# Two narrow attentions of a four-layer transformer: raw bank copied once, units turned in pairs, first sequences prepared in the stage before

## The reference, cut to what matters

```python
# layer 1: one k and v of 8 columns, shared by the 16 heads
latent = x @ Wc_down; q = (latent @ Wq_up).reshape(B, T, 16, 8)
k, v = split(latent @ Wkv_up)                    # causal softmax(q k / sqrt 8) @ v, then @ Wc_proj
# layer 3: k and v for every head, causal and no further back than 128 tokens
q, k, v = split(x @ w_in.T + b_in, 3)            # 16 heads of 8
allowed = (j <= i) & (j >= i - 128)
return (softmax(where(allowed, q k / sqrt 8, -1e9)) @ v) @ w_out.T + b_out
```

## Time and profile before

| | |
|---|---|
| three timed runs | 2560.18 us median (2559.87 to 2560.31) |
| the profiled execution | 2552.11 us, its span in the trace 2550.4 us |
| PE busy over the span | 92% |
| DVE, ACT, POOL busy | 63%, 58%, 63% |
| TensorE clock granted, mean | 0.976 |
| stage 2, last output of stage 1 to its own last output | about 858 to 1157 us |
| stage 6, likewise | about 2168 to 2503 us |

### The profile page before, as it was taken

How to read it: one execution, slowest core, us unless ns; L and a number is a source line. 1 busy time by engine, 2 the same in 40 slices (tenths; PEclk the granted TensorE clock), 3 DMA queues, 4 the chain that set the end, 5 groups by cost and what they waited for, 6 DMA issues and landing times. The chain is left out here.

```text
span 2550.4 us, 61619 instructions
## 1 busy us (share of the span) xinstructions
PE 2348.4 (92%) x23721; PEld 1820.9 (71%) x23721; DVE 1604.4 (63%) x4234; ACT 1470.3 (58%) x3038; POOL 1595.8 (63%) x2569
## 2 busy tenths in 40 slices
PE   6999999999998699988999999999999968788897
PEld 5888888888886366656777788777877757455555
DVE  5666666666664277774455477777777622577776
ACT  5666666666664377764444466666656523466665
POOL 6888888888884444443333277777777722566664
PEclk8999999999999789999999999999999989899999
DMA  8930000000000100001000000000000045000000
GB/s 295 328 129 2 2 2 2 2 2 2 2 2 1 40 7 2 2 2 33 1 1 1 3 4 4 6 6 6 4 6 6 4 145 172 15 10 8 8 4 34
DMA packets 22915, 82.91 MB, mean 33 GB/s; under 512 B 3969, under 2 KB 10882, under 8 KB 21602
## 3 DMA queue, kind: packets, MB, share of 16 engines
q1 hardware_dynamic: 19474, 71.76, 8.8%
q0 software_dynamic: 3152, 7.21, 0.9%
HBM read 71.76 MB, written 46.79 MB: 46 GB/s over the span
## 5 line engine op out<-in xcount | busy, mean ns | idle before, releaser
L978 POOL TENSOR_TENSOR XR<-XR,T 128x256 f32<-128x256 f32 x504 | 369.0, 732 | 36.9 <-DVE T L858 7.3
L722 ACT ACTIVATE P<-ps 128x384 f32<-128x384 f32 (+1 forms) x512 | 250.7, 542 | 179.9 <-PE ps L2691 178.4
L2691 PE MATMUL ps<-P,V 128*64 128x256 f32 (+3 forms) x4096 | 332.0, 345 | 9.2 <-DVE O L1482 7.9
L1466 DVE TENSOR_REDUCE bm<-ps 128x3 f32<-128x384 f32 x512 | 260.0, 549 | 105.5 <-PE ps L2691 104.6
L2691 PEld LDWEIGHTS ps<-P,V 128*64 128x64 f32 (+1 forms) x4096 | 185.5, 123 | 131.0 <-issue 44.7
L1401 ACT ACTIVATE P<-ps 128x768 f32<-128x768 f32 x256 | 207.7, 811 | 99.6 <-PE ps L2691 99.1
L889 DVE TENSOR_REDUCE sm<-ps 128x2 f32<-128x512 f32 (+1 forms) x256 | 129.9, 549 | 187.6 <-PE ps L2691 187.6
L1567 POOL TENSOR_SCALAR_AFFINE_SELECT P<-P 128x512 f32<-128x512 f32 x256 | 162.6, 635 | 119.1 <-ACT P L1401 116.3
L991 POOL TENSOR_TENSOR PS<-P 128x256 f32<-128x256 f32 x256 | 181.5, 734 | 70.7 <-ACT P L722 70.4
L2691 PE MATMUL ps<-mk,identb 128*128 128x256 bf16 (+1 forms) x1024 | 202.6, 292 | 14.4 <-DVE bm L1466 11.3
L1012 POOL TENSOR_TENSOR ss<-ss,nhalf 128x16 f32<-128x16 f32 x64 | 187.7, 2933 | 5.3
(11 more groups left out here) (310 smaller groups left out, 6853.2 us busy)
## 6 DMA issues: line engine op xcount, KB each, us to landing
rows_i<-in_zero SPq DMA_DIRECT2D x16, 1208.0 KB, 31.9
rows_o<-in_zero SPq DMA_DIRECT2D x16, 1208.0 KB, 81.8
w<-in_m_w SPq DMA_DIRECT2D x23, 578.0 KB, 4.1
zt<-rows_i SPq DMA_DIRECT2D x23, 128.0 KB, 3.2
rows_o<-yo POOLq DMA_DIRECT2D x23, 128.0 KB, 3.9
stg<-in_t_w SPq DMA_DIRECT2D x11, 256.0 KB, 2.8
XR<-in_x SPq DMA_DIRECT2D x4, 512.0 KB, 8.9
out<-XR SPq DMA_DIRECT2D x8, 256.0 KB, 2.0
```

What stands on the lines that cost most here:

```text
L722: e.activation(self.P[at % 6][:, :], K.ps.ap("st", s, g, h)[:, 0:self.w], ACT.Exp, bias=0.0, scale=1.0 if kind == 0 else 0.125).then_inc(K ...
L978: p = po.e.tensor_tensor(x, x, self.T[g % 2][:, par, pr], ALU.add)
L1466: e.tensor_reduce(bm[:, h, :], K.ps.ap("mx", s, g, h)[:, 0:384].rearrange("p (a c) -> p a c", c=128), X, ALU.max, negate=True).then_inc(K. ...
L2691: return self.te.matmul(o, l, r, start=start, stop=True, skip_group_check=True)
```

## The change

In both stages ACT copies the raw bank once, whole, into SBUF (`rf`), which frees the bank; the high and low parts are made from rf one tick later, in two instructions each instead of four, and a new semaphore `lo_in` tells PE that the low parts stand. Two units share one bank at k=18: PE transposes both, DVE has one reciprocal and one product of twice the size. On DVE the k=18 part now stands first in its tick and the first parts of prep last. In stage 6 (kind 3) ka is also turned for two units in one bank and copied by one ACT instruction of 512 columns; ACT writes each high part twice in one instruction, and POOL only clears the column, at prep k=4. In stage 2 (kind 1) the first two sequences are prepared in stage 1 (`Ffn0`), as `ahead` items at its ticks 16 and 17, with stage 1's ring of banks; every other item of stage 2 but the weight load starts 14 ticks earlier.

```diff
-            first = 14
+            first, lead = 14, 14
         else:
             self.tk = {"zT": 5, "raw": 8, "v": 9}
-            first = 11
+            first, lead = 11, 0
+        self.early = 2 if kind == 1 else 0
         items = []
         for b in range(NSEQ):
-            items.append((8 * b, 0, "prep", (b,), max(self.tk.values()) + 1))
+            if b >= self.early:
+                items.append((8 * b - lead, 0, "prep", (b,), max(self.tk.values()) + 1))
             for u in range(4):
-                items.append((8 * b + first + 2 * u, 1, "unit", (b, u), 19))
-            items.append((8 * b + first + 6 + 21, 2, "final", (b,), 4))
+                items.append((8 * b + first - lead + 2 * u, 1, "unit", (b, u), 19))
+            items.append((8 * b + first - lead + 6 + 21, 2, "final", (b,), 4))
         items += [(at, 3, "load", (ld,), ld.parts) for at, ld in loads]
-        items += [(128 + 6 * g, 4, "ahead", (s + 1, g), 6) for g in range(2)]
+        items += [(128 - lead + 6 * g, 4, "ahead", (s + 1, g), 6) for g in range(2)]
         self.order = ticks(items, lambda name, k: not (name == "unit" and k in (0, 6)))
-        self.dve_order = ticks(items, lambda name, k: not (name == "unit" and k in (3, 4)))
+        self.dve_order = ticks(items, self.dve_rank)
...
+        self.rf = sb(f"rf{s}", [128, 2, 144 if kind == 1 else 256], F32)
...
+    def dve_rank(self, name, k):
+
+        if name == "unit":
+            return 0 if k == 18 else 1 if k in (3, 4) else 2
+        return 3 if name == "prep" and k < 3 else 2
+
+    AHEAD = (0, 2, 5, 8, 11, 12, 14)
+
+    def ring(self, b):
+
+        return self.K.stages[self.s - 1].G if b < self.early else self.G
+
+    def early_pe(self, pe, b, k):
+        self.pe_prep(pe, b, self.AHEAD[k])
...
+    def early_pool(self, po, b, k):
+        if k == 0:
+            for n in range(2):
+                self.pool_clear(po, 2 * b + n)
+        self.pool_prep(po, b, self.AHEAD[k])
...
-        pe.wait_ge(*K.ps.read("raw", self.s, b))
+        pe.wait_ge(self.lo_in, b + 1)
...
+            if kind == 3 and u % 2 == 0:
+                ps = K.ps.take(pe, self.G, *self.kz_name(b, u))
+                for n in range(2):
+                    p = self.pe_turned(pe, ps[:, 256 * n:256 * n + 256], b,
+                                       self.ka[b % 3][:, :, 4 * (u + n):4 * (u + n) + 4, :])
+                p.then_inc(K.ps.full_of(*self.kz_name(b, u)), 1)
...
+        if k == 18 and u % 2:
+            ps = K.ps.take(pe, self.G, "pT", s, g // 2)
+            for n in range(2):
+                pe.wait_ge(*K.ps.read("pv", s, g - 1 + n))
+                for i in range(2):
+                    o = 256 * i + 128 * n
+                    p = K.tr(ps[:, o:o + 128], self.Ts[(g - 1 + n) % 4][:, 128 * i:128 * i + 128])
+            p.then_inc(K.ps.full_of("pT", s, g // 2), 1)
...
+            ps, o = K.ps.ap("raw", s, b), self.rf[:, :, :]
+            if kind == 1:
+                o, ps = o.rearrange("p t c -> p (t c)"), ps[:, 0:288]
+            else:
+                o, ps = o.rearrange("p n (t c) -> p n t c", t=2), ps[:, :].rearrange("p (t n c) -> p n t c", t=2, n=2)
+            e.activation(o, ps, ACT.Copy).then_inc(K.ps.out_of("raw", s, b), 1)
+        if k == tk["raw"] + 1:
             if b >= 3:
                 ac.wait_ge(*K.ps.filled("qq", s, 4 * (b - 3) + 3))
-            ac.wait_ge(*K.ps.filled("raw", s, b))
+            ac.wait_ge(*K.ps.read("raw", s, b))
             ac.wait_ge(*self.cleared(b))
             rq, rk = self.raw(b)
-            for t in range(2):
-                e.activation(self.qa[b % 3][:, t, :, 0:8], rq[:, t], ACT.Copy)
-            for t in range(2):
-                i = e.activation(self.ka[b % 3][:, t, :, 0:8], rk[:, t], ACT.Copy)
-            i.then_inc(self.hi_in, 1)
+            if kind == 3:
+                for a, r, step in ((self.qa, rq, 16), (self.ka, rk, 8)):
+                    i = e.activation(self.twice(a[b % 3], step), r.unsqueeze(2).to_broadcast([128, 32, 2, 8]), ACT.Copy)
+                i.then_inc(self.hi_in, 1)
...
+            e.tensor_tensor(self.cols(ka, 16), rk, fv(self.cols(ka, 0)), ALU.subtract)
+            e.tensor_tensor(self.cols(qa, 8), rq, fv(self.cols(qa, 0)), ALU.subtract).then_inc(self.lo_in, 1)
...
+    def pool_prep(self, po, b, k):
+
+        K, s = self.K, self.s
+        if k == 0:
+            for i in range(2):
+                K.pool_rstd(po, K.nb[s] + 2 * b + i)
+        if k == 1 and self.kind == 3 and b + 1 < NSEQ:
+            self.pool_back(po, b + 1)
+        if k == 4 and self.kind == 3:
+            if b >= 3:
+                po.wait_ge(*K.ps.filled("qq", s, 4 * (b - 3) + 3))
+            po.wait_ge(*self.cleared(b))
+            po.e.memset(fv(self.qa[b % 3][:, :, :, 24:25].rearrange("p t h c -> p (t h) c")), 0.0).then_inc(self.qk8, 1)
...
+        self.base(K, s, [(2 * g, 0, "group", (g,), 10) for g in range(8)] + [
+            (16 + b, 4, "ahead", (s + 1, b), 7) for b in range(2)], loads)
```

More of the change, by code:

```diff
@@ L1082, in __init__ @@
         self.order = ticks(items, lambda name, k: not (name == "unit" and k in (0, 6)))
-        self.dve_order = ticks(items, lambda name, k: not (name == "unit" and k in (3, 4)))
+        self.dve_order = ticks(items, self.dve_rank)
         sb = K.scratch
+        self.qq = [sb(f"qq{s}_{i}", [128, 512], F32R) for i in range(4)]
+        self.P = [sb(f"P{s}_{i}", [128, 2, 512], F32) for i in range(6)]
+        self.Ts = [sb(f"Ts{s}_{i}", [128, 256], F32) for i in range(4)]
+        self.clear, self.hi_in, self.qk8 = (K.sem(f"{n}{s}") for n in ("clear", "hi_in", "qk8"))
@@ L1085, in __init__ @@
+        self.lo_in = K.sem(f"lo_in{s}")
+        self.v_in, self.masked, self.least = K.sem(f"v_in{s}"), K.sem(f"masked{s}"), K.sem(f"least{s}")
         self.zT = [sb(f"zT{s}_{i}", [128, 256], F32) for i in range(2)]
         self.z = [sb(f"z{s}_{i}", [128, 2, 128], F32) for i in range(2)]
-        self.kz = [sb(f"kz{s}_{i}", [128, 256], F32R) for i in range(4 if kind == 1 else 8)]
-        self.qq = [sb(f"qq{s}_{i}", [128, 512], F32R) for i in range(4)]
-        self.bm = [sb(f"bm{s}_{i}", [128, 4, 3], F32) for i in range(2)]
@@ L1090, in __init__ @@
[L1090 to L1096 removed]
+        self.kz = [sb(f"kz{s}_{i}", [128, 256 if kind == 1 else 512], F32R) for i in range(4)]
@@ L1143, in pe_prep @@
         if k == tk["zT"]:
-            ps = K.ps.take(pe, self.G, "zT", s, b)
+            ps = K.ps.take(pe, self.ring(b), "zT", s, b)
             pe.wait_ge(K.zs, K.nb[s] + 2 * b + 2)
@@ L1149, in pe_prep @@
         if kind == 1 and k == tk["lt"]:
-            ps = K.ps.take(pe, self.G, "lt", s, b)
+            ps = K.ps.take(pe, self.ring(b), "lt", s, b)
             pe.wait_ge(*K.ps.read("zT", s, b))
@@ L1154, in pe_prep @@
         if kind == 1 and k == tk["raw"]:
-            ps = K.ps.take(pe, self.G, "raw", s, b)
+            ps = K.ps.take(pe, self.ring(b), "raw", s, b)
             pe.wait_ge(*K.ps.read("lt", s, b))
@@ L1172, in pe_prep @@
         if kind == 3 and k == tk["v"]:
-            ps = K.ps.take(pe, self.G, "v", s, b)
+            ps = K.ps.take(pe, self.ring(b), "v", s, b)
             for i in range(2):
@@ L1180, in pe_turn @@
         K = self.K
-        ps = K.ps.take(pe, self.G, *name)
+        ps = K.ps.take(pe, self.ring(b) if name[0] == "kz" else self.G, *name)
         self.pe_turned(pe, ps, b, parts).then_inc(K.ps.full_of(*name), 1)
@@ L1232, in pe_unit @@
             p.then_inc(K.ps.full_of("pv", s, g), 1)
-        if k == 18:
-            ps = K.ps.take(pe, self.G, "pT", s, g)
-            pe.wait_ge(*K.ps.read("pv", s, g))
-            for i in range(2):
-                p = K.tr(ps[:, 128 * i:128 * i + 128], self.Ts[g % 3][:, 128 * i:128 * i + 128])
-            p.then_inc(K.ps.full_of("pT", s, g), 1)
+        if k == 18 and u % 2:
[6 more added lines that the diff above has]
+            p.then_inc(K.ps.full_of("pT", s, g // 2), 1)
     def partner(self, b, u, k):
@@ L1290, in pe_final @@
             ps = K.ps.take(pe, self.G, "OT", s, b)
-            for u in range(4):
-                pe.wait_ge(*K.ps.read("pT", s, 4 * b + u))
+            for n in range(2):
+                pe.wait_ge(*K.ps.read("pT", s, 2 * b + n))
             for i in range(2):
@@ L1446, in dve_prep @@
                 K.dve_z(dv, n + i, self.z[b % 2][:, i, :], K.XR[:, 2 * b + i, :])
-        if k == tk["raw"]:
+        if k == tk["raw"] + 1:
             rq, rk = self.raw(b)
@@ L1787, in __init__ @@
     def __init__(self, K, s, loads=()):
-        self.base(K, s, [(2 * g, 0, "group", (g,), 10) for g in range(8)], loads)
+        self.base(K, s, [(2 * g, 0, "group", (g,), 10) for g in range(8)] + [
+            (16 + b, 4, "ahead", (s + 1, b), 7) for b in range(2)], loads)
         self.hf = [K.scratch(f"hf{s}_{i}", [128, 512], F32) for i in range(12)]
```

121 lines of the change are left out of this document (59 added, 62 removed).

## The result

The changed kernel takes **2497.1 us** (2492.2 to 2501.8, 4 runs) against 2560.0 of the kernel before beside it (2558.5 to 2560.3, 4 runs): ratio 0.9755, interval 0.9735 to 0.9775. I had forecast 2524 with a range down to 2500; it lies 2.9 us under that range. The profiled execution is the slowest of the four, 2501.75, span 2500.1; the one of before was quicker than its runs, 2552.1. From profile to profile it is 50.4 us, and that is what rows can divide.

The account below looks back on a forecast made before the run. It saw a sparse, low-clock start of stage 2, then PE nearly full but waiting for banks; -17 - 7 - 13 + 1 = -36 us gave 2516 profiled, 2524 timed with the 8.1 us offset, range 2500 to 2547.

Parts of the forecast that it names:

- Start of stage 2, -17: Seam of stages 1 and 2: preparing two sequences early gains 18.5 us, 1.3 given back; -17 if the clock stays up.
- my rounds of 4.83: Stage 2's weight load: chunks sharing a buffer lie 4.83 us apart, three such rounds before the first P,V product.
- Steady state of stage 2, -7: Stage 2 after its start: fewer bank waits over 15 sequences, -7 us (0 to -14).
- half of 0.93 as kept: Stage 2: PE's waits for O and q's low part cost 0.93 us a sequence; half of that counted as gained.
- Together 1.79 - 0.4 - 0.4, rounded down for 14 full sequences: -13 us: Stage 6: both bank waits gone, 1.79 us a sequence, less 0.4 for ACT's full tick and 0.4 for slower subtractions.
- Start of stage 6, +1: Stage 6's start is not prepared ahead and its first chain gets longer by copies: +1 us.
- It ran 8.1 us under the median: Kernel before: its profiled execution was 2552.1 us against 2560.2 timed; this offset was added to the forecast of 2516.
- every bank wait goes and nothing new comes: Rival for the whole kernel: -19 start, -14 stage 2, -27 stage 6, together -60, 2500 us; chance 0.14.
- PE meets the next late engine: Objection to the 2500 us rival: PE in its order meets another late engine, in stage 6 ACT's full tick.
- -5 for the stage: Stage 6 term instead of -13 if POOL held both subtractions each time and PE felt 1.0 us instead of 0.4.

Follow-up runs that it names:

- the second pair: Profiles of both kernels run again unchanged: the kernel before at 2557.4 us, the changed kernel at 2501.2 us, ratio 0.9775.

## Why the prediction was right and where it failed

- **Start of stage 2, -17.** The number is right, 16.8 in the profiles and about 17 by taking it away, and that is partly luck: I had 18.5 gained at the first P,V product and 1.3 given back, and it was 22.2 gained (908.03 to 885.85) and 5.4 given back. Stage 1 did grow by about 4 us (last yb turn 861.1 to 865.3 in kernels with early work, 857.8 to 861.9 without), first scores 863.85 for 865.4, first P,V 885.85 for 889.5. Two premises were wrong. The clock did not stay at 1.00, it was lost at 869. And the load does not set the pace from the scores to P,V: that took 22.0 us, not the 24.1 of my rounds of 4.83, and the same 22.0 with the load spread; in the kernel that keeps the clock by added masks (load spread, no pairing) it took 19.3.
- **Steady state of stage 2, -7.** 10.5 in the first pair of profiles, 14.4 in the second, at the upper end of my bounds. I counted "half of 0.93 as kept". The pace fell by 1.1 us a sequence, more than the whole 0.93, and the split was wrong: the order of DVE's work did it (16.0 to 14.9 alone, back to 15.6 when undone). The copy of the raw bank and the pairing replace each other, and both together are the slower choice: 14.5 us without pairing, 14.7 without rf, 14.9 with both.
- **Stage 6: the step that failed.** "Together 1.79 - 0.4 - 0.4, rounded down for 14 full sequences: -13 us". Measured 22.1, in the second pair 23.3. Neither 0.4 exists. The first, ScalarE's doubled copies held against PE, has the wrong sign: without them PE waits 1.2 us a sequence for POOL, and the stage is some 11 us longer. The second, the subtractions beside POOL, is small on DVE (0.27 us a sequence more for both, where I allowed 1.0), and PE feels nothing: no wait of PE in 192 us ends with a low part any more, and with the maxima only 0.5 us in all. So the whole 1.79 was gained and 0.1 on top, 1.9 us of pace. My 14 full sequences were too many, as ten gaps have this pace; 14 x 1.79 = 25 is nearer to 22.1 than 13 all the same.
- **Start of stage 6, +1.** -1.0 for all that lies between the stages' steady parts; it adds 2 us to the miss.
- **Sum.** Terms of -36 for a measured -50.4 make 14.4 of the miss of 27: 9.1 in stage 6, 3.5 in stage 2, 2.0 ahead of stage 6, less 0.2. The other 12.6, nearly half, is "It ran 8.1 us under the median": this offset belonged to one execution, not to the profile. Before's profile lay low by 6 to 8 us, and that of the changed kernel high by 3 to 5. Against 2516 for a profiled execution the kernel had 2501.75.
- **The rival that came nearest** is "every bank wait goes and nothing new comes": -60, 2500. Its parts were -19, -14, -27 for a measured 15.7 to 16.8, 10.5 to 14.4 and 22.1 to 23.3: its mechanism is what the rows show, its sum is 5 to 10 us too large from profile to profile, and within the 57.5 and 62.9 us that the medians of two groups give. I held against it that PE meets the next late engine; in the undo runs it does, but the change had removed that one too.
- **The Trainium skill's rule**, "SBUF — State Buffer", section "SBUF: two separate sides", which I gave -5 for the stage: the runs with the swapped subtractions and without rf agree with it (0.88 for 0.41 us; 2.62 for 0.17). That such a minimum stays out over five masks in a row, no run here takes apart. Whether it costs depends on who waits: in the changed kernel nobody, in the one without rf 1.96 us a sequence and the clock after it.

Still open: why the minima miss POOL's row of masks in the changed kernel (268 ns at most in stage 6) and hit it without rf or with the pairing alone; I take it for a matter of phase, but didn't vary that alone. Nor is the kernel with masks tripled (0.9730) told from the one without (0.9751) by its interval, and the latter, in another group, isn't told from the changed kernel's first 0.9755. What the raw copy is worth in stage 2 alone, on the kernel before, was not run.

## What to carry to other kernels

Ask for each wait which instruction is late and why, before asking which resource it holds: O was late for its place in DVE's tick, and on the kernel before, one sort key alone gave 22 us and the pairing, meant to save a bank, gave 5. Undo and do each part alone: prices of parts that replace each other don't add, and a copy that is booked as a cost may stand in for a slower one elsewhere. Take a profile's distance from its runs for chance until a second profile shows it again.
